# Decays in four SBUF places made a chunk ahead, input products in two PSUM places made in pairs, in a selective-scan layer on one core

## The reference, cut to what matters

```
A = -exp(A_log)                                   # 512 channels x 16 states
xp = x_hat @ x_proj_w.T;  d_rank, Bm, Cm = split(xp, 64, 16, 16)
delta = softplus(d_rank @ dt_proj_w + dt_proj_b)  # length x 512
deltaA = exp(delta * A)                           # "decay"
deltaB_u = delta * Bm * x_hat                     # "inp"
h = deltaA_t * h + deltaB_u_t                     # over 1024 steps, "hid"
y_t = sum over states of h * C_t                  # "ch", then summed
x1 = x + y + x_hat * D
```

## Time and profile before

| | |
|---|---|
| median of 3 runs | 4562.7 us (4562.11 to 4563.24) |
| the profiled execution | 4562.84 us, its span 4561.0 us |
| VectorE busy | 3848.1 us (84%) |
| GpSimd busy | 3434.3 us (75%) |
| TensorE busy | 2979.0 us (65%) |
| ScalarE busy | 2822.1 us (62%) |
| scans, first to last start | 80 us to 3,505 us |

### The profile page before, as it was taken

How to read it: one execution, slowest core, us unless ns; L and a number is a source line. 1 busy time by engine, 2 the same in 40 slices (tenths; PEclk the granted TensorE clock), 3 DMA queues, 4 the chain that set the end, 5 groups by cost and what they waited for, 6 DMA issues and landing times. The chain is left out here.

```text
span 4561.0 us, 60367 instructions
## 1 busy us (share of the span) xinstructions
PE 2979.0 (65%) x17062; PEld 1352.7 (30%) x17062; DVE 3848.1 (84%) x3098; ACT 2822.1 (62%) x4359; POOL 3434.3 (75%) x1748
## 2 busy tenths in 40 slices
PE   3666565656565656566665656565654289999997
PEld 1222222222222222222222222222222145555553
DVE  3999999999999999999999999999998745555442
ACT  5777776777767677767777777777665222322221
POOL 3999999999999999999999999999997100000010
PEclk7657565756565656566565656565655599999998
DMA  4454546364645545454545463646443300000000
GB/s 104 97 137 116 150 107 160 87 170 93 160 103 144 120 132 145 111 137 113 139 117 147 106 166 81 171 92 160 106 127 79 138 14 19 18 18 18 18 19 7
DMA packets 198220, 472.92 MB, mean 104 GB/s; under 512 B 60688, under 2 KB 61200, under 8 KB 197088
## 3 DMA queue, kind: packets, MB, share of 16 engines
q1 hardware_dynamic: 177136, 452.11, 39.3%
q0 software_dynamic: 20736, 16.88, 1.4%
HBM read 126.83 MB, written 73.43 MB: 44 GB/s over the span
## 5 line engine op out<-in xcount | busy, mean ns | idle before, releaser
L893 POOL TENSOR_TENSOR ch<-hid,cmat 128x1024 f32<-128x1024 f32 x1024 | 2390.3, 2364 | 95.8 <-DVE hid L762 72.6
L762 DVE TENSOR_TENSOR_SCAN hid<-decay,inp 128x1024 f32<-128x1024 f32 x1024 | 2273.8, 2275 | 95.8 <-ACT decay L613 90.1
L613 ACT ACTIVATE decay<-delr,a_neg 128x1024 f32<-128x1024 f32 x1024 | 1133.8, 1112 | 542.6 <-DVE hid L762 538.7
L404 PE MATMUL ps_y<-ch,nsum 128*32 128x256 f32 x8192 | 950.8, 564 | 763.8 <-POOL ch L893 762.6
L751 DVE TENSOR_TENSOR inp<-dx,bmat 128x1024 f32<-128x1024 f32 x880 | 1014.2, 1214 | 63.3 <-ACT dx L621 63.3
L404 PEld LDWEIGHTS ps_y<-ch,nsum 128*32 128x32 f32 x8192 | 251.9, 141 | 1433.4 <-POOL ch L893 1231.0
L415 PE MATMUL ps_y<-ident,ysb 128*128 128x128 f32 x1024 | 342.2, 434 | 364.4 <-ACT ysb L628 344.5
L415 PEld LDWEIGHTS ps_y<-ident,ysb 128*128 128x128 f32 x1024 | 249.0, 300 | 600.8 <-ACT ysb L628 552.1
L399 PE MATMUL ps_y<-xhT,dskip 128*32 128x256 f32 x2048 | 263.1, 605 | 208.8 <-ACT xr L635 208.8
L1146 POOL DMA_INDIRECT out_rows<-row,idx_out x16 | 41.1, 2570 | 400.0 <-issue 218.9
L858 POOL TENSOR_TENSOR inp<-dxr,bmat 128x1024 f32<-128x1024 f32 x144 | 339.8, 2360 | 0.0
(11 more groups left out here) (167 smaller groups left out, 3954.2 us busy)
## 6 DMA issues: line engine op xcount, KB each, us to landing
dxr<-dxT SPq DMA_DIRECT2D x1024, 128.0 KB, 2.4
delr<-delT SPq DMA_DIRECT2D x1024, 128.0 KB, 2.4
xr<-in_x SPq DMA_DIRECT2D x32, 1024.0 KB, 6.6
bmat<-b_and_c SPq DMA_DIRECT2D x256, 128.0 KB, 3.4
cmat<-b_and_c SPq DMA_DIRECT2D x256, 128.0 KB, 3.1
x_rows<-xr SPq DMA_DIRECT2D x16, 2048.0 KB, 7.6
out_rows<-xr SPq DMA_DIRECT2D x32, 1024.0 KB, 4.4
w<-in_w SPq DMA_DIRECT2D x2, 4096.0 KB, 24.5
```

Of the source, the lines that this page charges most:

```text
L404: last = pe.matmul(ps_y[q * CH:(q + 1) * CH, 0:2 * P], nsum[:], ch[:, g, q * 2 * P:(q + 1) * 2 * P], start=False, stop=(g == GROUPS - 1))
L613: nc.scalar.activation(decay[:, g % 2, :], delr[:, c % 2, :], ACT.Exp, scale=a_neg[:, i:i + 1])\
L762: nc.vector.tensor_tensor_scan(hid[:, g, :], decay[:, g % 2, :], inp[:, g, :], 0.0, ALU.mult, ALU.add).then_inc(hid_ready, 1)
L893: nc.gpsimd.tensor_tensor(ch[:, g, :], hid[:, g, :], cmat[:, g, :], ALU.mult).then_inc(ch_ready, 1)
```

## The change

`decay` goes from two places in PSUM to four in SBUF, and `inp` from four places in SBUF to two in PSUM. GpSimd's product of group 3 in the chunks of `OWN_AT` goes to SBUF as before, but now to `decay`'s place 3, and the decay of that tile is written to `inp`'s place 1 in PSUM, as a "late" decay, after scan (c, 1) has read that place. All other decays of chunk c+1 are made during chunk c, each as soon as the scan of its group in chunk c is done. VectorE's order within a chunk was four scans, then four products of the next chunk (three before a chunk of `OWN_AT`); now it is two scans, this chunk's products 2 and 3 (2 only in a chunk of `OWN_AT`), two scans, the next chunk's products 0 and 1.

```diff
-        decay = ps("decay", [P, 2, L])
+        inp = ps("inp", [P, 2, L])
-        inp = sb("inp", [P, GROUPS, L])
+        decay = sb("decay", [P, GROUPS, L])
+            def decays_done(b, c):
+                if c in OWN_AT:
+                    sp.wait_ge(late_decay, pool_inputs(b, c))
+                    sp.sem_inc(repeating, 1)
+                    sp.wait_ge(decay_ready, inputs(b, c, OWN - 1) + 1)
+                else:
+                    sp.wait_ge(decay_ready, inputs(b, c, OWN) + 1)
...
-                if has(b, 1) or c >= 2:
-                    sp.wait_ge(decay_ready, tile(b, c - 1, 0))
+                if c >= 2:
+                    decays_done(b, c - 2)
+                elif has(b, 1):
+                    decays_done(b - 1, c - 2 + CHUNKS)
...
             def exp_decay(b, c, g):
-                if has(b, 1) or c * GROUPS + g >= 2:
-                    act.wait_ge(hid_ready, tile(b, c, g) - 1)
                 if g == 0:
                     act.wait_ge(del_rep[c % 2], (b * (CHUNKS // 2) + c // 2 + 1) * 16 * NT)
                 i = c * GROUPS + g
-                nc.scalar.activation(decay[:, g % 2, :], delr[:, c % 2, :], ACT.Exp, scale=a_neg[:, i:i + 1])\
-                    .then_inc(decay_ready, 1)
+                if g == OWN and c in OWN_AT:
+                    act.wait_ge(hid_ready, tile(b, c, g) - 1)
+                    nc.scalar.activation(inp[:, 1, :], delr[:, c % 2, :], ACT.Exp, scale=a_neg[:, i:i + 1])\
+                        .then_inc(late_decay, 1)
+                else:
+                    if has(b, 1) or c >= 1:
+                        act.wait_ge(hid_ready, tile(b, c, g) - GROUPS + 1)
+                    nc.scalar.activation(decay[:, g, :], delr[:, c % 2, :], ACT.Exp, scale=a_neg[:, i:i + 1])\
+                        .then_inc(decay_ready, 1)
...
                 for c in range(CHUNKS):
                     nxt = (b, c + 1) if c < CHUNKS - 1 else (b + 1, 0)
+                    more = not (final and c == CHUNKS - 1)
+                    if more:
+                        exp_decay(*nxt, 0)
                     beside(b, par, c, 0)
-                    exp_decay(b, c, 2)
+                    if c in OWN_AT:
+                        exp_decay(b, c, OWN)
+                    if more:
+                        exp_decay(*nxt, 1)
...
-                    exp_decay(b, c, 3)
-                    if not (final and c == CHUNKS - 1):
+                    if more:
                         copy_dx(*nxt)
...
                     beside(b, par, c, 1)
-                    for g in (0, 1):
-                        if not (final and c == CHUNKS - 1):
-                            exp_decay(*nxt, g)
-                        beside(b, par, c, 2 + g)
+                    if more:
+                        exp_decay(*nxt, 2)
+                    beside(b, par, c, 2)
+                    if more and nxt[1] not in OWN_AT:
+                        exp_decay(*nxt, 3)
+                    beside(b, par, c, 3)
...
-                if has(b, 1) or c > 0:
-                    dve.wait_ge(hid_ready, tile(b, c, g) - GROUPS + 1)
-                nc.vector.tensor_tensor(inp[:, g, :], dx[:], bmat[:, g, :], ALU.mult).then_inc(inp_ready, 1)
+                if has(b, 1) or c > 0 or g >= 2:
+                    dve.wait_ge(hid_ready, tile(b, c, g) - 1)
+                nc.vector.tensor_tensor(inp[:, g % 2, :], dx[:], bmat[:, g, :], ALU.mult).then_inc(inp_ready, 1)
...
                 for c in range(CHUNKS):
-                    for g in range(GROUPS):
+                    for g in (0, 1):
+                        scan(b, c, g)
+                    for g in (2, 3):
+                        if not (g == OWN and c in OWN_AT):
+                            make_input(b, c, g)
+                    for g in (2, 3):
                         scan(b, c, g)
...
-                nc.gpsimd.tensor_tensor(inp[:, OWN, :], dxr[:, c % 2, :], bmat[:, OWN, :], ALU.mult)\
+                nc.gpsimd.tensor_tensor(decay[:, OWN, :], dxr[:, c % 2, :], bmat[:, OWN, :], ALU.mult)\
                     .then_inc(pool_input, 1)
```

More of the change, by code:

```diff
@@ L165, in scan_phase @@
         decay_ready = sem("decay_ready")
+        late_decay = sem("late_decay")
         inp_ready = sem("inp_ready")
@@ L660, in _ @@
                     copy_dx(0, 0)
-                    for g in range(2):
+                    for g in range(GROUPS):
                         exp_decay(0, 0, g)
@@ L747, in make_input @@
                     dve.wait_ge(b_in[g], (b + 1) * 16 * NT)
-                if has(b, 1) or c > 0:
-                    dve.wait_ge(hid_ready, tile(b, c, g) - GROUPS + 1)
-                nc.vector.tensor_tensor(inp[:, g, :], dx[:], bmat[:, g, :], ALU.mult).then_inc(inp_ready, 1)
+                if has(b, 1) or c > 0 or g >= 2:
+                    dve.wait_ge(hid_ready, tile(b, c, g) - 1)
+                nc.vector.tensor_tensor(inp[:, g % 2, :], dx[:], bmat[:, g, :], ALU.mult).then_inc(inp_ready, 1)
             def scan(b, c, g):
-                dve.wait_ge(decay_ready, tile(b, c, g) + 1)
+                factor, addend = decay[:, g, :], inp[:, g % 2, :]
                 if g == OWN and c in OWN_AT:
+                    factor, addend = addend, factor
+                    dve.wait_ge(late_decay, pool_inputs(b, c))
                     dve.wait_ge(pool_input, pool_inputs(b, c))
                 else:
+                    dve.wait_ge(decay_ready, inputs(b, c, g) + 1)
                     dve.wait_ge(inp_ready, inputs(b, c, g) + 1)
@@ L761, in scan @@
                     dve.wait_ge(ch_ready, tile(b, c, g) - GROUPS + 1)
-                nc.vector.tensor_tensor_scan(hid[:, g, :], decay[:, g % 2, :], inp[:, g, :],
+                nc.vector.tensor_tensor_scan(hid[:, g, :], factor, addend,
                                              0.0, ALU.mult, ALU.add).then_inc(hid_ready, 1)
@@ L783, in _ @@
                     .then_inc(dskip_ready, 1)
-            for g in range(GROUPS):
+            for g in range(2):
                 make_input(0, 0, g)
@@ L795, in body @@
                         router(b - 1, other, ROUTER.index(c))
-                    for g in range(GROUPS):
-                        if g == OWN and (c + 1) % CHUNKS in OWN_AT:
-                            continue
+                    for g in (0, 1):
                         if c < CHUNKS - 1:
```

## The result

The changed kernel takes 4590.61 us (median of 4 runs, 4588.48 to 4593.83) against 4562.4 us before: a ratio of 1.0062, interval 1.0045 to 1.0080. It is slower by 28 us, where 4579 us had been forecast (16 us slower). The profiled execution took 4593.83 us, its span is 4591.3 us; it is the slowest of the four, 31.0 us over the profiled execution of before.

The account below looks back on a forecast made before the run. GpSimd's work plus its idle stretch in chunk 4, decided by VectorE's chunks 0 to 3, bounds a batch. Even batches +12.2, odd −5.4, chunk 5 +9.6: +16.4 on 4562.7 gives 4579 us, range 4542 to 4604.

Parts of the forecast that it names:

- rival (c): SBUF and PSUM places cost 0.045 us on 14 products and 6 decays, 15 times: +13.5, 4593 us; chance 0.13.
- (d): ScalarE falls behind in chunk 6, holding VectorE or GpSimd 1 us more in each batch: 4594 us; chance 0.05.
- The wait for delr: At ScalarE's batch head, decay (1, 0) waits until +2.0; VectorE's first product of chunk 1 starts at +6.4, before +5.1.
- rival (a): Faster: GpSimd's idle stretch in chunk 4 closes, gaining 55 us: 4508 us; chance 0.15.
- GpSimd's wait in chunk 0: GpSimd's first delta step waits 1.5 us for the last softplus part, costing nothing while chunk 4's idle stretch is longer.
- Even batches: GpSimd starts product (4, 2) at +62.7 instead of +61.3: +1.35 us in each of nine batches, counting 1 and 15.
- Odd batches: GpSimd starts product (4, 2) at +62.7 instead of +63.6, the loop's turn being hidden: −0.9 us in each of six.
- Chunk 5: GpSimd waits about 0.6 us for a softplus part, counting in all 16 batches: +9.6 us.
- The one place of `dx`: copy_dx has two scans (4.4 us) instead of four; it fits in chunks 3 to 15, about 1 us spare in chunk 6.
- Memories: Decays written to SBUF and VectorE's products written to PSUM: between 0 and 0.045 us either way, taken as 0.
- A product that the next scan reads: On VectorE, scan (3, 2) directly follows the product it reads: start-to-start 1.25 us against 1.125, +0.12 us.
- Rival (b): No change to speak of: start as forecast, but chunk 5's softplus part is in time: +6.8, 4570 us; chance 0.22.

Follow-up runs that it names:

- e1: The changed kernel with SyncE issuing the next batch's dxr and delr of chunk 1 before cmat of groups 0 and 1: 4546.54 us.
- e2: The kernel before with SyncE issuing the next batch's dxr and delr of chunk 1 before cmat of groups 0 and 1: 4565.86 us.
- e4: The changed kernel, but in chunk 0 alone ScalarE makes decays (1, 0) and (1, 1) behind copy_dx of chunk 1, not ahead of copy_y: 4555.98 us.
- e3: The changed kernel with the last softplus part of chunk 5 moved from place 2 to place 1, before decay (6, 2): 4583.1 us.
- e9: The changed kernel with e1, e3, chunk 0's softplus parts and decay (1, 2) ahead of copy_x1, and chunk 2's dxr and delr issued before the loop's turn: 4527.02 us.

## Why the prediction was right, and by how much it was off

The sign, the range and the mechanism held. The time alone would not show it: 4590.6 us lies nearer to rival (c) with 4593 and to (d) with 4594 than to the forecast 4579. What decides between them are the rows, step by step:

- **What is removed**: right. VectorE's waits for decays went from 90.1 to 0.4 us.
- **The wait for delr**: right. ScalarE waits 141.7 us in 36 pieces. Forecast: `copy_dx` of chunk 1 ends at +6.35 and that of chunk 2 at +19.85; measured as means of even batches +6.6 and +20.1. e1, e2 and e4 show it as the cause from three sides: land it earlier, and 44 us go; in the other order it is worth nothing; take the queue out from behind it, and 35 go. One argument around it was too strong: against rival (a) it is said that no order on ScalarE changes when delr lands and that break-even needs delr at about +0.7. In e4 delr lands at +1.8 to +3.7, and the kernel is 7 us faster than before: it was enough that `copy_dx` did not stand behind the wait.
- **GpSimd's wait in chunk 0**: right in place, sized 1.5 us, measured 1.1 to 3.0 in batches 1 to 15. That it costs nothing behind a later idle stretch was not tested by itself.
- **Even batches**: forecast +1.35 us at product (4, 2), measured 63.05 − 61.45 = +1.6.
- **Odd batches: the term that was mis-sized.** "In the changed kernel the turn lies under ScalarE's wait and under a `copy_y` that comes 4 us later, so I take +62.7 again." In the six batches 3 to 13 that a turn precedes, product (4, 2) starts at +64.2 as a mean, where it was +64.0: +0.2 and not −0.9. The turn of TensorE did hide (`copy_x1` waits 1.24 us in batch 7, against 4.63 in e1), but delr landed at +4.1 to +4.9 in batches 3, 7 and 13, and product (4, 2) there at +65.0 to +65.8. In batches 5, 9 and 11 delr landed at +2.0 to +2.2 and the product at +62.9 to +63.1, close to the forecast. In batch 7 ScalarE's wait ended at 1601.99, +5.0.

The forecast was 16.4 us over before, the profiled execution 31.0. Of these 14.6 us the six odd batches are 6.5, the nine like even ones (+1.67 us each against 1.35) 2.9, and chunk 5 is 1.0; the rest was not followed up.

ScalarE in batch 7 of the changed kernel (first product at 1596.98), and SyncE's queue just before:

```profile
1601.99 1.15 ACT L632 ACTIVATE decay<-delr,a_neg 128x1024 f32<-128x1024 f32 x1 [10.25 <-DMA delr<-delT]
```

```profile
1592.40 3.15 SPq L274 DMA_DIRECT2D dxr<-dxT  x4
1595.60 2.50 SPq L280 DMA_DIRECT2D delr<-delT  x4
```

The landing of these four DMAs of delr, and then of those of batch 6:

```profile
DMA to landing us min/median/max: 2.4/2.6/4.4
```

```profile
DMA to landing us min/median/max: 2.4/2.4/2.5
```

Three of the four land as quickly as ever, and the last takes 4.4 us from issue to landing instead of some 2.5 (3.9 us in batch 3, 4.2 in batch 13). The issues start late as well: the four of dxr take 3.15 us where those of the earlier trace rows take 2.44. But that is no mark of these batches: in batch 6 they take 3.36 us, and delr lands at +2.7. Nor does the late last DMA come from the change: the kernel before has it in batch 3 (3.7 us, landed at +3.7), where nothing waited for it; e3 has it in batches 5 and 11 and e4 in batch 3. In these traces it is always a batch behind the loop's turn, and not always the same one. Why is open: no run was made for it.

- **Chunk 5**: forecast 0.6 us, measured 0.56 to 0.74 in 16 batches, and e3 gives 7.5 us back for it.
- **The one place of `dx`**: "in chunks 3 to 15 it fits by the same counting" was wrong for chunk 8, where `copy_dx` holds VectorE 0.7 to 1.7 us in 15 batches. It cost nothing because GpSimd was behind, not because the copy fitted.
- **Memories**: the late decays still go to PSUM, so one run has both: 1113 ns there, 1142 into SBUF. VectorE's product takes 1217 ns into PSUM, 1214 before into SBUF.

The groups by line of the changed kernel, from 150 to 3700 us:

```profile
L632 ACT ACTIVATE decay<-delr,a_neg 128x1024 f32<-128x1024 f32 x858 | 973.4, 1142 | 290.0 <-DVE hid L791 149.8 <-DMA delr<-delT 140.1
...
L626 ACT ACTIVATE inp<-delr,a_neg 128x1024 f32<-128x1024 f32 x143 | 159.1, 1113 | 52.7 <-DVE hid L791 51.3
```

The two sizes taken at 0 are 0.03 us for a decay into SBUF and 0.003 us for a product into PSUM. As an estimate, with the forecast's 6 decays and 14 products and 15 batches they come to 3 us, where rival (c) asked for 13.5; (c) is out but for that. The prediction's own comparison, 1011 against 1056 ns, was between a copy and an exponential, and the decay into PSUM with its 1112 ns did not fit it; the two lines above compare the same function. So the direction that the Trainium skill gives for ScalarE ("PSUM — Partial Sum Buffer", Specifications) agrees, at 0.03 us. For VectorE, the estimate of 0.065 us did not come. The two rows of the Trainium skill that it was taken from ("VectorE: DVE Perf Modes", The TRN2 errata) differ in where an instruction reads, not in where it writes, so this measurement does not speak against them.

- **A product that the next scan reads**: forecast +0.12 us, shown by 1423.81 to 1425.11, 1.30 us, against 1.13 before a scan that reads another product: +0.17, in 143 such pairs (1.295 to 1.303 us). The wait for a result is not free here. The Trainium skill ("VectorE: DVE Perf Modes", The DRAIN you can't avoid) measured for a chain of copies that a semaphore costs nothing extra, and this pair does not agree; the same section says that an instruction that is not held starts earlier, and with that the 1.13 us agree.

Rival (a), the idle stretch in chunk 4 closing, did not come even in e9: in even batches GpSimd still starts product (4, 2) some 1.6 us late. VectorE's own work, products and routers included, is what is left there. Rival (b) fell with the wait in chunk 5. Of (d) only the harmless part came: ScalarE did fall behind, at the copy for chunk 8, but its late decays held VectorE for 2.7 us in the whole launch, and GpSimd waited for no scan there. The sign "odd and even batches alike in length" held in part: they differ by 0.9 us as means (217.3 and 216.4 us), before by 1.9, and the difference is that of batches 3, 7 and 13.

## What to carry to other kernels

When an instruction is moved ahead in an in-order engine's program, look at every wait that it brings along, and price what stands behind it, not the instruction: here decays were made earlier so that nobody would wait for them, and the first of them held the one copy that the next engine needed. Making work ahead also asks for its inputs a step earlier: the DMA queue's order has to move with it (one swap there turned a loss of 28 us into a gain of 17). In a loop over two batches, the batch behind the turn runs by other times than the other, and a chain costed on one kind alone misses.

## What the runs showed of the hardware that had not been expected

Of the four 128 KB DMAs of delr, the last took 3.9 to 4.4 us from issue to landing in three batches behind the loop's turn, where all others of the changed kernel in this place took 2.3 to 3.2 us. In e1, where they are issued some 7 us earlier, all of them took 3.8 to 4.6 us, in every batch.

The turn of the loop costs each engine another time, and shows only where nothing covers it: TensorE's made `copy_x1` wait 4.1 to 4.9 us instead of 1.25 (e1), VectorE's left it idle for 2.5 to 3.0 us before scan (0, 0) in the changed kernel and for at most 0.31 us in the kernel before. VectorE's writes of 1024 elements to PSUM and to SBUF differ by 3 ns, ScalarE's by 29.
